# Output projections of a four-layer Flamingo block: norm applied by ScalarE, low parts by VectorE, updates ahead of turned tiles, first up products moved into two projections

## What is computed

```python
    x = x + jnp.tanh(g_xattn[2]) * _L2_xattn_ref(_layernorm(x, axis=-1), ctx_512, ...)
    x = x + jnp.tanh(g_ffn[2]) * _L2_ffn_ref(_layernorm(x, axis=-1), L2_ffn_gate_w, ...)
```

```python
            for e in range(E):
                g = h @ w_gate[e].T
                u = h @ w_up[e].T
                out = jax.nn.silu(g) * u @ w_down[e].T
                y = y + cw[:, e:e + 1].astype(x.dtype) * out
```

## Time and profile before

| | before |
|---|---|
| median of 3 runs | 2444.45 us (2442.24 to 2446.96) |
| profiled execution, its own time | 2444.12 us |
| its span, first to last instruction | 2442.3 us |
| PE busy, share of the chain that ended last | 2272.5 us (93%), 83% |
| DVE busy | 1572.0 us (64%) |
| POOL busy | 1399.5 us (57%) |
| ACT busy | 1038.7 us (43%) |
| mean granted clock of TensorE | 0.946 |

### The profile page before, as it was taken

One profiled execution on the slowest core, in us unless ns is written; L12 is line 12 of the kernel. 1 busy time (PEld: TensorE's weight loads), 2 busy tenths in 40 slices (PEclk: granted clock), 3 DMA queues, 4 the chain that ended last, 5 costly groups with the idle time before them and its releaser, 6 DMA issues.

```text
span 2442.3 us, 31169 instructions
## 1 busy us (share of the span) xinstructions
PE 2272.5 (93%) x11544; PEld 1575.6 (65%) x11544; DVE 1572.0 (64%) x2552; ACT 1038.7 (43%) x1518; POOL 1399.5 (57%) x859
## 2 busy tenths in 40 slices
PE   6889999899999995699999999989997999999988
PEld 5677887666666662465566666577786666666676
DVE  4666652378787867765777878652224788787652
ACT  3443443355555533311355555433332555555433
POOL 0342200178888872256588888734342688888743
PEclk9899999799999997699799999989998999999989
DMA  1025564111111013100111111022211111111010
...
DMA packets 49842, 136.48 MB, mean 56 GB/s; under 512 B 7469, under 2 KB 13437, under 8 KB 49244
## 3 DMA queue, kind: packets, MB, share of 16 engines
...
## 4 chain that ended last, share of the span: by engine, by line
PE 83%; DVE 8%; ACT 2%; issue 2%; POOL 2%; DMA 1%; PEld 0%; POOLq 0%; SPq 0%; PEldq 0%; DVEq 0%; ACTq 0%
PE psum L867 22%; PE psum L1287 18%; PE psum L1258 10%; PE psum L1277 10%; PE psum L1279 10%; PE psum L1454 2%; PE psum L1304 2%; PE psum L1409 2%; PE psum L1377 1%; PE psum L1185 1%; PE psum L1477 1%; DMA V<-in_ctx 1%; PE psum L1094 1%; PE psum L1074 1%; DVE mx L2191 1%
## 5 line engine op out<-in xcount | busy, mean ns | idle before, releaser
L2191 DVE TENSOR_REDUCE mx<-psum 128x1 f32<-128x500 f32 x1008 | 652.0, 675 | 235.5 <-PE psum L1258 223.8
L1699 ACT ACTIVATE E<-psum 125x896 f32<-125x896 f32 x576 | 528.1, 920 | 590.5 <-PE psum L1279 562.8
L1953 POOL TENSOR_TENSOR SA<-SA,E 125x896 f32<-125x896 f32 x282 | 597.4, 2118 | 22.1
L1287 PE MATMUL psum<-E,V 125*64 125x448 f32 x2304 | 472.2, 545 | 0.0
L1258 PE MATMUL psum<-K,Q 128*128 128x500 f32 x1008 | 360.4, 413 | 20.8 <-ACT Q L1686 11.2
L1277 PE MATMUL psum<-Q,K 128*125 128x448 f32 x1152 | 333.1, 370 | 2.3 <-ACT E L1699 2.3
L1279 PE MATMUL psum<-Q,K 128*125 128x448 f32 x1152 | 331.3, 369 | 0.0
L1287 PEld LDWEIGHTS psum<-E,V 125*64 125x64 f32 x2304 | 152.9, 136 | 231.0 <-issue 223.4
L1258 PEld LDWEIGHTS psum<-K,Q 128*128 128x128 f32 x1008 | 190.1, 192 | 165.3 <-issue 45.2
L1953 POOL TENSOR_TENSOR SA<-SA,SB 125x896 f32<-125x896 f32 x93 | 194.1, 2087 | 156.0 <-DVE SB L2212 156.0
L1277 PEld LDWEIGHTS psum<-Q,K 128*125 128x125 f32 x1152 | 214.1, 188 | 37.3 <-ACT E L1699 6.9
...
## 6 DMA issues: line engine op xcount, KB each, us to landing
...
```

Source lines behind the costliest of these rows:

```text
L1287: i = e.matmul(psum[c * DC:(c + 1) * DC, 4 + b % 2, 0:HT], V[0:LP, b, k * DC:(k + 1) * DC], E[g[n, b, k] % NE][0:LP, half[c]], start=k == ...
L1699: e.activation(E[m % NE][0:LP, :].rearrange("p (c q) -> p c q", c=2), psum[0:LP, pair:pair + 2, 0:HT], ACT.Exp).then_inc(exp_set.sem, 1)
L1953: e.tensor_tensor(SA[b % 2][0:LP, :], a[0:LP, :], x[0:LP, :], ALU.add).then_inc(sum_set.sem, 1)
L2191: e.tensor_reduce(mx[:, b % 2, j * 3 + c:j * 3 + c + 1], psum[:, bank, 0:CW], AX.X, ALU.max).then_inc(small_free.sem, 1)
```

## The change

- `act_apply` (new) applies the norm on ACT as `scale * x + bias` with `rstd` and `shift`, one row operand each; `dve_apply` leaves the projections. `shift` is minus the mean times `rstd`: DVE negates the mean in `dve_stats`, POOL multiplies behind its power (`pool_scales`, new).
- `low_by_pool`: in layers 2 and 3 only tile 0's low part stays on POOL; the others go to DVE. Layers 0 and 1 keep theirs.
- In `dve_project` the update of `X` and its statistics come ahead of the turned tile (`dve_turn`) of the same step. `dve_router` moves to step 1 in layers 2 and 3.
- The splits of the first two weight blocks move to steps 3 and 4 on both engines, on ACT to the end of the step.
- `pe_up` (new, cut out of `pe_experts`): in layers 2 and 3 `up` 0, 0 is made within the projection, behind logits 4 in layer 2 and logits 3 in layer 3 (`EARLY_UP`), into banks 1 and 2. Its place in the round of banks 4 to 7 goes, so later uses have other banks.
- The selector's copy to `selr` moves from DVE, ahead of `GT`, to ACT, at `("route", 1)`, which in ACT's order lies between R of `up` 0, 0 and R of `up` 0, 1.
- `shift` takes 28 bytes of each partition, which move the tiles behind it.

```diff
@@ -361,6 +361,7 @@
 TURN_BEHIND = {0: 2, 1: 0, 2: 2, 3: 4}
+EARLY_UP = {2: 5, 3: 4}
 TURNED_NORM = {0: 1, 2: 5, 3: 8}
@@ -370,6 +371,8 @@
     for t in order:
+        if t == ("up", 0, 0) and SWIGLU[f]:
+            continue
         if t[0] == "up":
@@ -422,6 +425,7 @@
     rstd = mem.take("rstd", [P, NT], F32)
+    shift = mem.take("shift", [P, NT], F32)
     folded_at = mem.at
@@ -732,7 +736,7 @@
 
-        return n == 1 or i % 2 == 0 or (n, i) == (3, 3)
+        return n == 1 or i == 0 or (n == 0 and i % 2 == 0)
 
@@ -852,6 +856,8 @@
             upper_before[f, use] = upper_free(f, uses[m - 4]) if m >= 4 else None
+        for k in range(2 if f in (2, 3) else 0):
+            upper_bank[f, ("up", 0, 0, k)], upper_before[f, ("up", 0, 0, k)] = 1 + k, x_out.at(f, 4 + k)
 
@@ -1320,6 +1326,8 @@
                 pe_logits(e, n, i - behind - 1)
+            if n in (2, 3) and i - behind == EARLY_UP[n]:
+                pe_up(e, n, 0, 0)
             if n == 1 and i == 3:
@@ -1343,6 +1351,18 @@
 
+    def pe_up(e, f, n, c):
+        m, k = ffn[f], n % 4
+        if c == 0:
+            e.wait_ge(*wl_set.at(f, n))
+        for s in range(2 if SWIGLU[f] else 1):
+            bank = upper(e, f, "up", n, c, s)
+            pairs = []
+            for kd in range(KD):
+                o = slice(s * D + kd * P, s * D + (kd + 1) * P)
+                pairs += split_pairs(m["WH"][k][:, o], m["WL"][k][:, o], YH[:, kd, half[c]], YL[:, kd, half[c]])
+            product(e, psum[:, bank, 0:HT], pairs).then_inc(up_out.sem, 1)
+
     def pe_experts(e, f):
@@ -1350,17 +1370,8 @@
             if kind == "up":
-                n, c = t
-                k = n % 4
-                if c == 0:
-                    e.wait_ge(*wl_set.at(f, n))
-                for s in range(2 if swiglu else 1):
-                    bank = upper(e, f, "up", n, c, s)
-                    pairs = []
-                    for kd in range(KD):
-                        o = slice(s * D + kd * P, s * D + (kd + 1) * P)
-                        pairs += split_pairs(m["WH"][k][:, o], m["WL"][k][:, o], YH[:, kd, half[c]], YL[:, kd, half[c]])
-                    product(e, psum[:, bank, 0:HT], pairs).then_inc(up_out.sem, 1)
+                if not swiglu or t != [0, 0]:
+                    pe_up(e, f, *t)
             elif kind == "gate" and t[0] >= free:
@@ -1729,12 +1740,21 @@
                 act_part(e, n, i + 2)
-            if n != 1 and i in (4, 5):
-                act_split(e, n, i - 4)
+            if 0 <= i - 1 < NT:
+                act_apply(e, n, i - 1)
             if n == 3 and 0 <= i - 1 < NT:
                 act_square(e, i - 1)
             if behind and i >= behind:
                 act_project_turn(e, n, i - behind)
+            if n != 1 and i in (3, 4):
+                act_split(e, n, i - 3)
+        if n == 1:
+            act_apply(e, n, NT - 1)
+
+    def act_apply(e, n, i):
+
+        e.wait_ge(*rstd_set.at(1 + 2 * n, i))
+        e.activation(Y[:, i, :], X[:, i, :], ACT.Identity, scale=rstd[:, i:i + 1], bias=shift[:, i:i + 1]).then_inc(y_set.sem, 1)
 
@@ -1781,6 +1801,9 @@
                 e.activation(m["HH"][x % 4][:, :], m["HF"][x % 4][:, :], ACT.Copy).then_inc(hh_set.sem, 1)
+            elif kind == "route" and f != 0 and t[0] == 1:
+                e.wait_ge(*sel_in.at(f))
+                e.activation(m["selr"][:, :], m["sel"][:, :], ACT.Copy).then_inc(sel_set.sem, 1)
             elif kind == "route" and t[0] == 0:
@@ -1908,6 +1931,13 @@
 
+    def pool_scales(e, r, i):
+
+        e.wait_ge(*var_set.at(r, i))
+        e.tensor_tensor(rstd[:, i:i + 1], rstd[:, i:i + 1], exponent[:, 0:1], ALU.pow).then_inc(*pool_own.up())
+        e.wait_ge(*pool_own.now())
+        e.tensor_tensor(shift[:, i:i + 1], shift[:, i:i + 1], rstd[:, i:i + 1], ALU.mult).then_inc(rstd_set.sem, 1)
+
     def pool_core(e, n):
@@ -1969,9 +1999,9 @@
                 low_part(e, n, i + 2)
-            pool_rstd(e, 1 + 2 * n, i)
-            if n != 1 and i in (5, 6):
-                pool_split(e, n, i - 5)
+            pool_scales(e, 1 + 2 * n, i)
+            if n != 1 and i in (3, 4):
+                pool_split(e, n, i - 3)
             if n == 3 and i >= 2:
@@ -2068,6 +2098,8 @@
         e.wait_ge(*dve_own.now())
+        if r in (1, 3, 5, 7):
+            e.tensor_scalar(shift[:, i:i + 1], mv[:, i, 0:1], -1.0, None, ALU.mult)
         e.tensor_scalar(rstd[:, i:i + 1], mv[:, i, 1:2], 1e-5, None, ALU.add).then_inc(var_set.sem, 1)
@@ -2257,24 +2289,20 @@
                 low_part(e, n, i + 2)
-            if n != 3 and behind and 0 <= i - behind < NT:
-                dve_turn(e, r, i - behind, 4 + (i - behind) % 4)
             if i < NT:
                 e.wait_ge(*projected.at(n, i))
                 e.scalar_tensor_tensor(X[:, i, :], psum[:, i % 3, 0:D], tanh_g[:, n:n + 1], X[:, i, :], ALU.mult,
                                        ALU.add).then_inc(x_out.sem, 1)
                 e.wait_ge(*x_out.at(n, i))
                 dve_stats(e, r, i)
-            if 0 <= i - 1 < NT:
-                dve_apply(e, r, i - 1)
+            if n != 3 and behind and 0 <= i - behind < NT:
+                dve_turn(e, r, i - behind, 4 + (i - behind) % 4)
             if n == 3:
                 dve_rms(e, i)
             if n == 1 and i < 6:
                 dve_ternary(e, i)
-            if n != 1 and i == 3:
+            if n != 1 and i == (3 if n == 0 else 1):
                 dve_router(e, n)
-        if n == 1:
-            dve_apply(e, r, NT - 1)
 
@@ -2411,8 +2439,6 @@
         if step == 2:
-            e.wait_ge(*sel_in.at(f))
-            e.tensor_copy(m["selr"][:, :], m["sel"][:, :]).then_inc(sel_set.sem, 1)
             dve_gates(e, f)
```

## The result

The changed kernel takes 2433.91 us (2430.12 to 2438.49, 10 runs) against 2444.14 (2433.34 to 2449.51, 10 runs): ratio 0.9959, 95% interval 0.9944 to 0.9974, about 10 us less. Measured a second time, on a chip where before's median was 2440.14, the ratio was 0.9971 (0.9953 to 0.9990), 7 us less.

The account below looks back on a forecast made before the run. PE was taken as busy nearly throughout, with gains or losses only in the four projections and the gated expert heads. Layers 0 to 3 summed -0.8 - 0.5 - 3.6 + 1.0 = -3.9 us on 2444.1: 2440.2, range 2435.5 to 2446.

Parts of the forecast that it names:

- layer 0: First projection: earlier update gains 0.8, split leaving the path 1.26, against shift 0.55 and later last product 0.6; sum -0.8.
- layer 1: Second projection, VectorE the bound: -1.75 for applies moved off it, against negations, shift and ScalarE's apply; sum -0.5.
- layer 2, product phase: Third projection to product 6: router low part's stall gone, -2.8, and the half clock behind it, -1.2.
- layer 2, tail: After layer 2's last product: 12 up matmuls added, clock falling within them, 9.7 us against 8.5; +1.2.
- layer 2, head: Start of layer 2's experts: ScalarE stands for the selector's load, yet the first gate matmul comes 0.8 us earlier.
- layer 3, product phase: Fourth projection to product 6: logits 0 still wait for z2, its power behind POOL's second split; nothing booked.
- layer 3, tail: After layer 3's last product, PE the bound without gaps: 12 up matmuls add their full time; +3.2.
- layer 3, head: Start of layer 3's experts: turn of the gates at +7.9 us instead of 10.1, w clear of the split; -2.2.
- the stall on the router's low part: Layer 2's projection: PE's wait for the router's low part, 2.8 us, disappears with the router's parts made at step 1.
- clock high: Rival, chance 0.28: moved up matmuls lift the clock before both tails end; layer 3 -1, layer 2 -6, 2436 us.
- Wait moved: Rival, chance 0.20: selector-load stand and PE's idle time in the heads give back the projections' gains; 2443.3 us.
- Table load: Rival, chance 0.06: ScalarE's apply needs two table loads a tile, 6 us more in three projections, 2.6 in layer 1; 2461.

Follow-up runs that it names:

- e5_norm_dve: Changed kernel with the norm applied by VectorE again, no shift, POOL making only the power: 2438.79 us, ratio to before 0.9978.
- e10: Kernel before with only the update of X and its statistics moved ahead of the turned tile (layers 0 and 2): 2444.73 us, ratio 1.0022.
- e7: Changed kernel with the first two weight blocks' splits back at steps 4 and 5 (ScalarE), 5 and 6 (POOL): 2437.09 us, ratio to before 0.9974.
- e14: Kernel before with router at step 1, update ahead of the turned tile, and splits at steps 3 and 4: 2439.00 us, ratio 0.9981.
- e13: Kernel before with router at step 1 (layers 2, 3) and update ahead of the turned tile (layers 0, 2): 2437.21 us, ratio 0.9974.
- e6: Changed kernel with the low parts of layers 2 and 3 back on POOL as before: 2433.07 us, ratio to before 0.9968.
- e1: Kernel before with only the router's parts moved to step 1 in layers 2 and 3: 2436.85 us, ratio 0.9974.
- e11: Changed kernel without early up products, selector's copy one place later on ScalarE, layer 3's splits later: 2427.76 us, ratio to before 0.9949.

## Why the prediction was right and wrong

In order of its own steps, with the two profiles of the changed kernel against before:

| step | forecast | measured |
|---|---|---|
| layer 0 | -0.8 | -2.1, -2.7 |
| layer 1 | -0.5 | -1.1, -0.8 |
| layer 2, product phase | -4.0 | -5.1, -5.0 |
| layer 2, tail | +1.2 | -1.0, +0.6 |
| layer 2, head | -0.8 | -0.2, -1.2 |
| layer 3, product phase | 0 | -0.9, -0.2 |
| layer 3, tail | +3.2 | +2.2, +1.2 |
| layer 3, head | -2.2 | -2.0, -2.0 |
| sum | -3.9 | -10.2, -10.2 |

No single step makes the 6.3 us between the two sums: nearly every cost booked against a saving came smaller than booked or not at all, and several savings were not booked.

**Right:** the stall on the router's low part and the clock behind it; ScalarE's apply without table loads; VectorE as layer 1's bound; `w` clear of POOL's split; ScalarE's stand at the selector's load; the up products as full cost in layer 3's tail, 4.6 us in one profile and 4.1 in the other. The rows for ScalarE's apply in the changed kernel, by shape, and for the POOL pair:

```profile
L1757 ACT ACTIVATE Y<-X,shift,rstd 128x256 f32<-128x256 f32 x28 | 16.8, 599 | 54.7 <-POOL shift L1939 54.7
```

```profile
L1937 POOL TENSOR_TENSOR rstd<-rstd,exponent 128x1 f32<-128x1 f32 x28 | 25.4, 908 | 54.6 <-DVE rstd L2103 54.6
...
L1939 POOL TENSOR_TENSOR shift<-shift,rstd 128x1 f32<-128x1 f32 x28 | 8.9, 319 | 2.2
```

The apply took 0.599 us where I had 0.55, within its bounds. By the Trainium skill ("ScalarE: Activation LUTs", What ACT_TABLE_LOAD costs) it would be 0.585; the trace agrees to 0.014. The Trainium skill (same page, Rules for kernel authors) gives multiplication and addition to VectorE. For one operation alone the rows agree, 0.41 us on VectorE against 0.599; for this kernel it was the worse choice, since e5_norm_dve, which follows it, lost 3.8 us over the stretches.

**Wrong, and by what:**

*Layer 0.* Both savings were there as written: the update's 0.8 (0.7 in e10) and the split's 1.26 (e7 gives 0.9 to 1.4 back, e14 takes 1.6). But against them I had set 0.55 for `shift` and 0.6 for a later last product. In the tail `shift` takes 0.19, with a hop of 0.08, while the power before it is 0.10 shorter: 0.17 in all. And product 6 ends 23.6 and 23.05 us after product 0, 23.69 before: the split ahead of CL(6) delayed nothing that PE waited for. So 1.0 of the 1.15 us of cost didn't come, out of a miss of 1.3 to 1.9; the earlier end of product 6 and a sum rounded from -0.9 to -0.8 are most of the rest. The nearest row for `shift` was a power, and a multiplication is not one.

*Layer 1.* `shift` again. From the last variance to the last apply's end 0.34 us came on top where I had 0.69 (0.55 for `shift` and 0.14 for the apply); the last variance itself came 1.34 earlier, counted from product 0, where I had 1.15.

*Layer 2.* Three things. The half clock is worth 1.8, not 1.2. The update ahead of the turned tile is worth 1.1 to 1.3 in its tail (e10, e13); I had priced it for layer 0 alone and not carried it to the other layer with a turn 2 behind. And between e14's 23.22 and the 22.65 to 22.83 of all later kernels lie 0.4 to 0.6 us: the faster pace of the matmuls, since the seven products of e6 together are 0.54 shorter than those of e14. I had put the moved tiles at nothing without a reason. The clock in the tail is a matter of the execution: the first profile had it high (the rival's case), the six others with the up products there had a tail of 8.75 to 9.03.

*Layer 3.* The step that failed most by its reasoning is "I book nothing up to product 6". The sentence before it names the wait, logits 0 for the power of z2 behind POOL's second split, and then gives it no price. The early splits cost 2.7 to 3.3 us there (e7), 1.7 of it by that very wait and 1.55 by ScalarE's split and the longer low part. It looked like nothing because terms of the other sign lie beside it, none of them booked: ScalarE's norm, worth 2.5 to 2.8 us over the layer (e5), and the faster pace. In the rows PE waits 1.9 us longer up to product 6 and is busy 2.8 us less (23.8 against 26.6, at a clock of 0.89 against 0.84). That the result is only 0.2 to 0.9 from the forecast 0 is luck. The second step is "its tail has no gap": the earlier trace rows begins 5.4 us behind product 6, and in those 5.4 us PE had waited 3.9 for YL. In the changed kernel it waits 2.4, so 1.4 of the up matmuls' 4.6 were paid by waits that fell away, and the clock that came back behind them (half of the clock high rival) gave the rest: +2.2 and +1.2 for +3.2.

So the ledger of the four stretches, built up: before 183.65; router to 179.1 (e1 with layer 3 by e13, since its own was lucky: 32.75 + 40.03 + 46.72 + 59.58); update to 176.5; splits to 174.7; norm, low parts, selector and the moved tiles to 169.8; early up products back up to 173.5. Without the moved up products the change would be 3.7 us better there.

That POOL and VectorE hold each other up shows in the rows: 2.21 us for a low part of 0.19 (e10) and 1.53 for a power of 0.55 (the changed kernel). It is told by the Trainium skill too ("SBUF — State Buffer", Who interferes with whom): the two share one pair of ports, and an instruction keeps it until its end. The rows agree.

**The rivals.** *Clock high* (2436) came nearest, and its numbers nearly came: layer 2 -6.4 and -5.6 for its -6, layer 3 -0.7 and -1.1 for its -1. But that is mostly luck: the clock was high all through layer 2's tail in one profile of two and never all through layer 3's, and the rest of the gain came from the terms above. *Wait moved* had its mechanism right, the stand was there in both profiles and cost 2.3 to 3.3 us in the head; the projections had simply won more than it could give back. *Table load*: none stands beside the 28 applies, the changed kernel has its eight loads where before had them. (Its 6 us a projection were not worked out: 0.6 us a tile over seven tiles are 4.2.)

**Left open.** The stretch from layer 2's gate matmul to layer 3's product 0, edited by nobody, was 669.0 to 669.1 in three profiles with before's layer 2 and 664.7 to 670.7 in the others, 666.2 and 666.9 in the changed kernel. This could be an effect of where the edited stages leave the clock, or luck; no run separates the two, nor does any run hold the clock constant. From layer 0 to layer 1 the changed kernel drew the longer times, by 2 us on the mean of two profiles each. Open too are whether the place of the tiles sets the pace of the matmuls, and why the totals of e7, e10, e11 and e14 stand 3 to 5 us above what their stretches say.
